# Adjacency loads of a two-layer graph attention kernel issued one row group at a time between GpSimd's node steps

## The chip, the core and the metric

One core of a Trainium2 chip runs the whole program. The metric is the device time of one execution in microseconds; the times given are of several executions of the same program, and lower is better.

## What is computed

Two graph attention layers with a pre-norm and a residual, over 8192 nodes of 128 features and one dense 0/1 adjacency of 8192 x 8192 int32 (268 MB):

```python
h = jnp.maximum(_layernorm(x, axis=-1), 0.0)
x = x + layer(h, adj, W, b, a)          # twice, with each layer's own weights
# layer:
Wh = h @ W + b
e = leaky_relu((Wh @ a1)[:, None] + (Wh @ a2)[None, :], 0.2)
attention = softmax(where(adj > 0, e, -9e15), axis=1)
return attention @ Wh
```

The adjacency is the same in both layers.

## The kernel before, in words

**The work of a tile.** Both layers go through 64 tiles of 128 target nodes. Since a leaky ReLU has two branches, a score's exponential is one of two products of a factor of the row and a factor of the column; so a tile needs only two masks of bits (edge and positive score, edge and negative score) and 128 matmuls (L560) of these masks, read as fp8, with 64 chunks of prepared node rows (`node_rows`), into two PSUM banks. VectorE makes the masks: two of four score signs (`z_sign`, L831), the AND with the edges (`mask_bits`, L846), the packing of the edges for layer 1 (`pack`, L872 and L875), a transposition (`turn_bits`, L884) and two splits (`split_g1`, `split_g2`, L891). ScalarE makes the other two score signs (L635) and, in layer 0 alone, turns the adjacency from int32 to an int8 sign (`cast`, L622, from `adj_sb` into `sign_a`). Layer 1 uses the packed edges and loads no adjacency.

**The adjacency's tile.** A tile of the adjacency, 128 rows of 8192 int32, is 4 MB and comes as four row groups r = 0 to 3 of 1 MB, each an indexed DMA on GpSimd's queue (`load_adj`, L422) that gathers 128 pieces of 2048 numbers. `adj_sb` has one place for each row group and no second one, so the load of group r of one tile may start once ScalarE has cast group r of the tile before (`cast_done`). After its four loads GpSimd steps the index (`adj_index`, L428).

**Node steps.** During layer 0, behind the matmuls of tile T+2, the nodes of tile T are prepared for layer 1. The chain goes over all engines: VectorE's mean and `centred` (L745) and `var_eps` (L748); GpSimd's `rstd` (`node_step`, L438); TensorE's transposition (`turn`, L507, at chunk 8 of 64) and projection (`project`, L512, at chunk 24); between them ScalarE's copy (`node_copy`, L597); then VectorE's `ext` (L812); then GpSimd's sum and copy of the two scores (`h_sum` L450 and `nat` L451), ScalarE's factors and first product (`node_high`, L608 and L610), GpSimd's second product (`row_parts`, L460), and VectorE's two remainders (`node_low`, L819), the first of which waits for ScalarE's product and the second for GpSimd's. SyncE stores the rows.

**The orders.** Every engine's order is written out by hand and repeats tile by tile. ScalarE, in the tile T+2 of layer 0, goes: `part_a` of the tile before (L641, waits for its matmuls), cast r = 0 of tile T+4, `node_copy` of T, z sign, cast r = 1, z sign, cast r = 2, `node_high` of T, cast r = 3. VectorE goes: z sign, `part_ac` (L911, waits for `part_a`), z sign, `joined`, `mask_bits`, `empty`, `pack`, `den` and `numer`, `turn_bits`, `ext` of T, `rden`, `split_g1`, `x_new`, `split_g2`, `stats` (L732), first `node_low` of T, `mean_var`, second `node_low` of T, `centred` and `var_eps` of T+1. GpSimd goes, for the nodes of T, through `load_adj` of all four groups of tile T+4, `node_step`, then `node_rest`, which has the sums and the second product. `sweep` (L91 to L105) writes 4 tiles out, loops over the middle and writes the last out.

Of the kernel before, what the change touches and what calls it, by code (L numbers as in the profile page):

```python
# [28 lines left out]
TILES = NODES // TILE  # L29
QUADS = 4  # L30
QROWS = 32
SPAN = NODES // QUADS
RGROUPS = TILE // QROWS
# [29 lines left out]
HEAD = 4  # L63
TAIL = 60
NODE_STEP = 4
LOADS_AHEAD = 4


class Tile:
# [24 lines left out]
def sweep(eng, body, trail=0, step=2, head=HEAD, tail=None):  # L94

    end = TILES - (tail or step)
    for k in range(head):
        body(Tile(k))
    with eng.Fori(head // step, end // step) as u:
        for k in range(step):  # L100
            body(Tile(k, u, step))
    for k in range(end, TILES + trail):
        body(Tile(k))


def gat_kernel(nc, x, adj, w_0, b_w_0, a_vec_0, b_a_0, w_1, b_w_1, a_1, out):
# [10 lines left out]
    with ExitStack() as ctx:  # L117
        def sb(name, shape, dt):
            return ctx.enter_context(nc.sbuf_tensor(name, shape, dt))
# [4 lines left out]
        def sem(name):  # L124
            return ctx.enter_context(nc.semaphore(name))


        adj_sb = sb("adj_sb", [128, RGROUPS, SPAN], I32)
        adj_index = sb("adj_index", [128, 2, RGROUPS], I32)
# [72 lines left out]
        adj_loaded = [sem(f"adj_loaded_{r}") for r in range(RGROUPS)]  # L202
        cast_done, index_ready = sem("cast_done"), sem("index_ready")
# [32 lines left out]
        def row_slot(l, T):  # L236

            return (T.p4, T.n4) if l == 0 else (T.p, T.n)
# [146 lines left out]
        @block.gpsimd  # L385
        def _(pool):
            pool.memset(minus_half[:], -0.5).then_inc(ident_ready, 1)
            pool.memset(averager[:], 1.0 / NODES).then_inc(ident_ready, 1)
            pool.memset(ident[:], 0.0).then_inc(ident_ready, 1)
            pool.wait_ge(ident_ready, 3)  # L390
            pool.affine_select(out=ident[:], in_=ident[:], compare_op=ALU.not_equal, fill=1.0, base=0,
                               pattern=[[-1, 128]], channel_multiplier=1).then_inc(ident_ready, 1)
            pool.wait_ge(ident_ready, 4)
            t_columns = ident[:, TILES:2 * TILES].rearrange("p (a b) -> p b a", a=QUADS)

            def build_picks():
                for r in range(RGROUPS):
                    pool.tensor_copy(pick_s[:, r, :].rearrange("p (a i) -> p a i", a=QUADS),
                                     ident[:, QROWS * r:QROWS * (r + 1)].unsqueeze(1).to_broadcast([128, QUADS, QROWS])) \
                        .then_inc(picks_ready, 1)  # L400
                for b in range(BLOCKS):
                    pool.tensor_copy(pick_t[:, b, :].rearrange("p (a i) -> p a i", a=QUADS),
                                     t_columns[:, b, :].unsqueeze(2).to_broadcast([128, QUADS, QROWS])).then_inc(picks_ready, 1)

            build_picks()
            pool.iota(adj_index[:].rearrange("p b r -> p (b r)"), pattern=[[QUADS * TILE, 2], [QUADS * QROWS, RGROUPS]], base=0,
                      channel_multiplier=QUADS).then_inc(index_ready, 1)
            pool.wait_ge(index_ready, 1)
            for a in range(1, QUADS):
                part = adj_index[QROWS * a:QROWS * (a + 1), :, :].rearrange("p b r -> p (b r)")  # L410
                pool.tensor_scalar(part, part, float(a - QUADS * QROWS * a), 1.0, ALU.add, ALU.mult).then_inc(index_ready, 1)
                pool.wait_ge(index_ready, a + 1)
            adj_rows_of_2048 = adj.rearrange("n (a c) -> (n a) c", a=QUADS)

            def load_adj(T):

                pool.wait_ge(index_ready, QUADS + T.t)
                for r in range(RGROUPS):
                    if T.u is not None or T.k:
                        pool.wait_ge(cast_done, RGROUPS * (T.t - 1) + r + 1)  # L420
                    pool.nop(nofuse=True)
                    pool.indirect_dma_start(out=adj_sb[:, r, :], out_offset=None, in_=adj_rows_of_2048,  # L422
                                            in_offset=bass.IndirectOffsetOnAxis(ap=adj_index[:, T.p, r:r + 1], axis=0)) \
                        .then_inc(adj_loaded[r], 16)
                if T.u is None and T.k == 0:
                    pool.engine_nop().then_inc(index_ready, 1)
                else:
                    pool.tensor_scalar(adj_index[:, 1 - T.p, :], adj_index[:, 1 - T.p, :], float(2 * QUADS * TILE), 1.0,  # L428
                                       ALU.add, ALU.mult).then_inc(index_ready, 1)

            nat_v = nat[:].rearrange("p (c t) -> p c t", c=2)

            def node_step(l, T):

                pool.wait_ge(S[l].var_eps, T.t + 1)
                T.wait_before(pool, S[l].ext, 2)
                pool.nop(nofuse=True)
                pool.tensor_tensor(rstd[:, T.p, :], var_eps[:, T.p, :], minus_half[:], ALU.pow).then_inc(S[l].rstd, 1)  # L438

            def node_rest(l, T):  # L440

                pool.wait_ge(S[l].ext, T.t + 1)
                if T.u is None and T.k == 0:
                    if l:
                        pool.wait_ge(S[0].h_mean, 1)
                    pool.tensor_copy(h_sum[:], ext[:, T.p, 0:DIM]).then_inc(S[l].h_sum, 1)
                else:
                    pool.wait_ge(S[l].h_sum, T.t)
                    pool.nop(nofuse=True)
                    pool.tensor_tensor(h_sum[:], h_sum[:], ext[:, T.p, 0:DIM], ALU.add).then_inc(S[l].h_sum, 1)  # L450
                pool.tensor_copy(nat_v[:, :, ds(T.t, 1)], ext[:, T.p, NEG_S:POS_T + 1].rearrange("p (c o) -> p c o", o=1)) \  # L451
                    .then_inc(S[l].st_kept, 1)
                if l == 0:
                    return
                pool.wait_ge(S[l].b_and_d, T.t + 1)
                slot, used = row_slot(l, T)
                if T.u is not None or used:
                    pool.wait_ge(S[l].rows_stored[slot], 16 * used)
                pool.nop(nofuse=True)
                pool.tensor_scalar(row_parts[:, slot, ROW:ROW + PART], ext[:, T.p, 0:PART], b_and_d[:, T.p, 1:2], 1.0,  # L460
                                   ALU.mult, ALU.mult).then_inc(S[l].high_d, 1)

            for l in range(LAYERS):
                if l:
                    load_adj(Tile(1))
                    pool.wait_ge(S[0].nat_ps, 1)
                    pool.wait_ge(S[0].coefs, 2)
                    pool.wait_ge(limits, n_limits)
                    for k in range(2, LOADS_AHEAD):
                        load_adj(Tile(k))  # L470

                def body(T):
                    if l and T.u is None and T.k == TILES - 2:
                        pool.wait_ge(S[0].turned, TILES)
                        build_picks()
                    if l == 0 and T.u is None and T.k == HEAD - 1:
                        load_adj(Tile(0))
                    if l and T.plus(LOADS_AHEAD).exists:
                        load_adj(T.plus(LOADS_AHEAD))
                    if T.exists:  # L480
                        node_step(l, T)
                    rest = T.plus(l - 1)
                    if rest.exists:
                        node_rest(l, rest)

                sweep(pool, body, trail=1 - l, step=[NODE_STEP, 2][l], tail=[NODE_STEP, LOADS_AHEAD][l])


        @block.tensor
# [804 lines left out]
```

## Time and profile before

| | us |
|---|---|
| median of 3 executions | 2281.99 |
| lowest, highest | 2279.98, 2282.03 |
| the profiled execution, its own time | 2267.0 |
| its span, first to last instruction | 2265.1 |
| layer 0's matmuls, about | 205 to 1310 of the span |
| layer 1's matmuls, about | 1335 to 2256 of the span |

| engine | busy us of the span |
|---|---|
| TensorE, matmul | 2016.6 (89%) |
| VectorE | 1778.2 (79%) |
| ScalarE | 1123.6 (50%) |
| GpSimd | 762.0 (34%) |

The busy shares are means over both layers, and the layers differ: only layer 0 has adjacency loads, casts and node steps. So the rows below are taken mainly from the stretch 280 to 1240 us, where layer 0 repeats itself tile by tile, and from single tiles in it. A release in square brackets at the end of a timeline row says how long the engine stood idle before the instruction and what it then waited for.

### The profile page before, as it was taken

The page shows a single profiled execution, that of the slowest core. Times are in us where ns is not written, and L with a number is a line of the kernel's source. Part 1 is how long each engine was busy: PE and PEld are TensorE (multiplying, and loading weights), DVE is VectorE, ACT ScalarE, POOL GpSimd, SP SyncE. Part 2 cuts the span into 40 slices and gives each one's busy share as a digit, 9 for nine tenths or more (in the row PEclk, how much of TensorE's full clock was granted, in tenths as well). Part 3 has the DMA queues.
Part 4 walks back from the last instruction along what each step waited for, and adds up shares of the span by engine and source line. Part 5 has one row for each costly group of instructions (what it writes and reads, how often), then busy time and mean ns, then how long its engine had stood idle before and what let it go on. Part 6 is the DMA issues. An engine that isn't in the chain of part 4 may idle for free.

```text
span 2265.1 us, 46517 instructions
## 1 busy us (share of the span) xinstructions
PE 2016.6 (89%) x16866; PEld 1708.1 (75%) x16866; DVE 1778.2 (79%) x2733; ACT 1123.6 (50%) x1097; POOL 762.0 (34%) x819
## 2 busy tenths in 40 slices
PE   4558888888888988889898969999999999999998
PEld 2337777777767777777777858888888888888887
DVE  5668787877778777787877768888888888888885
ACT  3467666676666766667676433332222222333331
POOL 5655565555656655565555410000000000000000
PEclk9999999999999999999999989999999999999999
DMA  5558777766777776776766570000000000000000
GB/s 184 138 170 284 262 271 271 270 239 257 266 263 270 268 264 256 263 276 261 273 259 258 197 164 29 28 28 28 28 28 28 28 28 28 28 28 28 27 27 11
DMA packets 104788, 357.40 MB, mean 158 GB/s; under 512 B 12336, under 2 KB 61744, under 8 KB 67888
## 3 DMA queue, kind: packets, MB, share of 16 engines
q0 software_dynamic: 36864, 268.45, 31.2%
q1 hardware_dynamic: 65584, 71.73, 11.3%
q10 hardware_dynamic: 2304, 16.78, 2.3%
q8 instruction: 18, 0.29, 0.1%
q14 instruction: 18, 0.15, 0.0%
HBM read 314.84 MB, written 42.07 MB: 158 GB/s over the span
## 4 chain that ended last, share of the span: by engine, by line
PE 47%; DMA 19%; ACT 14%; issue 14%; DVE 3%; POOL 1%; POOLq 0%; SPq 0%; DVEq 0%; ACTq 0%
PE acc L560 46%; DMA adj_sb<-in_adj_dram,adj_index 17%; ACT sign_a L622 8%; ACT sign_z L635 4%; DMA node_rows<-row_parts 2%; POOL adj_sb L422 1%; DMA masks<-in_x_dram 1%; ACT centred_t L597 1%; DVE ext L812 1%; PE ps_h L512 1%; PE acc L529 0%; ACT b_and_d L608 0%; DVE sign_z L846 0%; DVE masks L884 0%; ACT row_parts L610 0%
## 5 line engine op out<-in xcount | busy, mean ns | idle before, releaser
L560 PE MATMUL acc<-node_rows,masks 128*128 128x258 f16 x16384 | 1896.4, 277 | 26.0 <-DVE masks L891 13.0
L560 PEld LDWEIGHTS acc<-node_rows,masks 128*128 128x128 fp8e4 x16384 | 1622.8, 99 | 282.4 <-issue 16.4
L622 ACT ACTIVATE sign_a<-adj_sb 128x2048 int8<-128x2048 int32 x256 | 486.1, 1900 | 305.0 <-DMA adj_sb<-in_adj_dram,adj_index 300.7
L635 ACT ACTIVATE sign_z<-t_row,neg_s 128x2048 int8<-128x2048 f32 x256 | 503.9, 1994 | 2.0 <-DVE masks L884 1.9
L422 POOL DMA_INDIRECT adj_sb<-in_adj_dram,adj_index x256 | 447.3, 1747 | 121.6 <-issue 94.6
L641 ACT ACTIVATE part_a<-acc,coef_a 128x258 f32<-128x258 f32 x128 | 60.2, 471 | 710.1 <-PE acc L560 701.0
L831 DVE TENSOR_SCALAR sign_z<-t_row,neg_s 128x2048 int8<-128x2048 f32 x256 | 327.0, 1279 | 2.9 <-issue 2.4
L891 DVE TENSOR_SCALAR masks<-masks 128x2048 uint32<-128x2048 uint32 x256 | 311.7, 1217 | 0.3
L884 DVE STREAM_TRANSPOSE masks<-sign_z 128x2048 uint32<-128x2048 uint32 x128 | 294.9, 2304 | 0.1
L512 PE MATMUL ps_h<-w_ext,centred_t 128*128 128x133 f32 x256 | 85.8, 430 | 180.1 <-ACT centred_t L597 172.7
L819 DVE SCALAR_TENSOR_TENSOR row_parts<-ext,b_and_d,row_parts 128x129 f16<-128x129 f32 x256 | 90.4, 355 | 176.6 <-ACT row_parts L610 176.2
L911 DVE SCALAR_TENSOR_TENSOR part_ac<-acc,coef_c,part_a 128x258 f32<-128x258 f32 x128 | 62.1, 485 | 208.4 <-ACT part_a L641 202.7
L512 PEld LDWEIGHTS ps_h<-w_ext,centred_t 128*128 128x128 f32 x256 | 54.0, 263 | 211.5 <-ACT centred_t L597 159.8
L450 POOL TENSOR_TENSOR h_sum<-h_sum,ext 128x128 f32<-128x128 f32 x126 | 113.2, 899 | 191.8 <-DVE ext L812 188.1
L846 DVE SCALAR_TENSOR_TENSOR sign_z<-sign_z,pair_a 128x2048 uint32<-128x2048 uint32 x64 | 146.5, 2289 | 6.1 <-DVE pair_a L855 2.9
L846 DVE SCALAR_TENSOR_TENSOR sign_z<-sign_z,sign_a 128x2048 uint32<-128x2048 uint32 x64 | 146.3, 2285 | 3.5 <-ACT sign_z L635 3.2
L875 DVE SCALAR_TENSOR_TENSOR pair_a<-sign_a,pair_a 128x2048 uint32<-128x2048 uint32 x48 | 109.5, 2282 | 0.0
L460 POOL TENSOR_SCALAR row_parts<-ext,b_and_d 128x129 f16<-128x129 f32 x64 | 26.4, 412 | 211.4 <-ACT b_and_d L608 211.4
L438 POOL TENSOR_TENSOR rstd<-var_eps,minus_half 128x1 f32<-128x1 f32 x128 | 92.8, 726 | 10.1 <-DVE var_eps L748 4.8
L812 DVE SCALAR_TENSOR_TENSOR ext<-ps_h,rstd,bias 128x133 f32<-128x133 f32 x128 | 43.0, 336 | 36.5 <-PE ps_h L512 35.8
L608 ACT ACTIVATE b_and_d<-ext 128x2 f32<-128x2 f32 x128 | 25.3, 198 | 82.5 <-DVE ext L812 41.8
L507 PE MATMUL ps_t<-ident,centred 128*128 128x128 f32 x128 | 47.4, 372 | 19.6 <-DVE centred L745 18.3
(87 smaller groups left out, 695.5 us busy)
## 6 DMA issues: line engine op xcount, KB each, us to landing
node_rows<-row_parts SPq DMA_DIRECT2D x128, 129.0 KB, 2.2
node_rows<-node_rows SPq DMA_DIRECT2D x32, 516.0 KB, 11.7
mask_bytes<-pair_a ACTq DMA_DIRECT2D x16, 1024.0 KB, 4.9
pair_a<-mask_bytes SPq DMA_DIRECT2D x16, 1024.0 KB, 4.8
adj_sb<-in_adj_dram,adj_index POOLq DMA_INDIRECT x256, 9.0
x_old<-in_x_dram SPq DMA_DIRECT2D x64, 64.0 KB, 2.5
x_after_layer<-x_new SPq DMA_DIRECT2D x64, 64.0 KB, 2.9
x_old<-x_after_layer SPq DMA_DIRECT2D x64, 64.0 KB, 1.8
```

Source lines behind the costliest of these rows:

```text
L422: pool.indirect_dma_start(out=adj_sb[:, r, :], out_offset=None, in_=adj_rows_of_2048, in_offset=bass.IndirectOffsetOnAxis(ap=adj_index[:, ...
L438: pool.tensor_tensor(rstd[:, T.p, :], var_eps[:, T.p, :], minus_half[:], ALU.pow).then_inc(S[l].rstd, 1)
L450: pool.tensor_tensor(h_sum[:], h_sum[:], ext[:, T.p, 0:DIM], ALU.add).then_inc(S[l].h_sum, 1)
L512: pe.matmul(ps_h[:, 0:EXT], centred_t[:, T.p, :], w_ext[l][:], start=True, stop=True).then_inc(S[l].h_raw, 1)
L560: mm = pe.matmul(acc[T.p][s][:, 0:ROW], stationary[s][:, c // BYTES, c % BYTES, :], node_rows[:, c, ROW * s:ROW * (s + 1)], start=(c == 0) ...
L622: nc.scalar.activation(sign_a[:, T.p, SPAN * r:SPAN * (r + 1)], adj_sb[:, r, :], ACT.Sign, scale=-1.0) \
L635: nc.scalar.activation(sign_z[:, T.p, SPAN * r:SPAN * (r + 1)], t_row[:], ACT.Sign, scale=-1.0, bias=neg_s[:, ds(RGROUPS * T.t + r, 1)]).t ...
L831: nc.vector.tensor_scalar(sign_z[:, T.p, SPAN * r:SPAN * (r + 1)], t_row[:], neg_s[:, ds(RGROUPS * T.t + r, 1)], -1.0, ALU.is_gt, ALU.mult) \
L846: nc.vector.scalar_tensor_tensor(out=bits, in0=bits, scalar=LOW_Z_WORD[l][T.p4], in1=edges, op0=ALU.bitwise_xor, op1=ALU.bitwise_and).then ...
L875: nc.vector.scalar_tensor_tensor(out=pair, in0=edges, scalar=KEEP_WORD[T.p4], in1=pair, op0=ALU.bitwise_and, op1=ALU.bitwise_or).then_inc( ...
L884: nc.vector.transpose(g2[:, T.p, :].bitcast(U32).rearrange("p (b r i) -> p r b i", r=RGROUPS, i=QROWS), sign_z[:, T.p, :].bitcast(U32).rea ...
L891: return nc.vector.tensor_scalar(out, words, abs(left), EDGE_WORD, shift, ALU.bitwise_and)
```

## The change

`load_adj` now loads one row group and the step of the index is a function of its own. In layer 0, GpSimd's order for the nodes of T becomes: `node_step`, load r = 0 of tile T+5, the sums, loads r = 1 and r = 2, the second product (`node_high`), load r = 3, the step of the index. Tiles 1 to 4 are loaded before the first node step, in one piece each; before, these were tiles 1 to 3, and the load of tile 4 stood directly ahead of that node step. The waits of each load on the cast before it are the same as they were. The sweep for the first nodes, before layer 0, keeps its order, and the tail of the layer's sweep is written out for one pair of tiles more.

```diff
-LOADS_AHEAD = 4
+LOADS_AHEAD = 5
...
-            def load_adj(T):
-
-                pool.wait_ge(index_ready, QUADS + T.t)
-                for r in range(RGROUPS):
-                    if T.u is not None or T.k:
-                        pool.wait_ge(cast_done, RGROUPS * (T.t - 1) + r + 1)
-                    pool.nop(nofuse=True)
-                    pool.indirect_dma_start(out=adj_sb[:, r, :], out_offset=None, in_=adj_rows_of_2048,
-                                            in_offset=bass.IndirectOffsetOnAxis(ap=adj_index[:, T.p, r:r + 1], axis=0)) \
-                        .then_inc(adj_loaded[r], 16)
+            def load_adj(T, r):
+
+                if r == 0:
+                    pool.wait_ge(index_ready, QUADS + T.t)
+                if T.u is not None or T.k:
+                    pool.wait_ge(cast_done, RGROUPS * (T.t - 1) + r + 1)
+                pool.nop(nofuse=True)
+                pool.indirect_dma_start(out=adj_sb[:, r, :], out_offset=None, in_=adj_rows_of_2048,
+                                        in_offset=bass.IndirectOffsetOnAxis(ap=adj_index[:, T.p, r:r + 1], axis=0)) \
+                    .then_inc(adj_loaded[r], 16)
+
+            def advance_index(T):
...
+            def load_all(T):
+                for r in range(RGROUPS):
+                    load_adj(T, r)
+                advance_index(T)
...
-                def body(T):
...
-                    if l and T.plus(LOADS_AHEAD).exists:
-                        load_adj(T.plus(LOADS_AHEAD))
-                    if T.exists:
-                        node_step(l, T)
-                    rest = T.plus(l - 1)
-                    if rest.exists:
-                        node_rest(l, rest)
...
+                def layer_0_tile(T):
...
+                    later = T.plus(LOADS_AHEAD)
+                    node_step(1, T)
+                    if later.exists:
+                        load_adj(later, 0)
+                    node_sums(1, T)
+                    if later.exists:
+                        load_adj(later, 1)
+                        load_adj(later, 2)
+                    node_high(1, T)
+                    if later.exists:
+                        load_adj(later, 3)
+                        advance_index(later)
```

GpSimd's order in the loop over layer 0's tiles, before (the second of the loop's two tiles; `REGISTER_ALU` rows set up addresses, and names ending in `_1` in the brackets are the semaphores of layer 1's nodes):

```order
L458 REGISTER_ALU [waits b_and_d_1]
L460 TENSOR_SCALAR row_parts<-ext,b_and_d 128x129 [waits rows_stored_1_0]
L417 REGISTER_ALU
L420 ISA [waits index_ready]
L422 DMA adj_sb<-in_adj_dram,adj_index 128x2048 [waits cast_done]
L420 REGISTER_ALU
L422 DMA adj_sb<-in_adj_dram,adj_index 128x2048 [waits cast_done]
L420 REGISTER_ALU
L422 DMA adj_sb<-in_adj_dram,adj_index 128x2048 [waits cast_done]
L420 REGISTER_ALU
L422 DMA adj_sb<-in_adj_dram,adj_index 128x2048 [waits cast_done]
L428 TENSOR_SCALAR adj_index<-adj_index 128x4
```

All four loads stand behind the second product of the tile before, which waits for ScalarE's `b_and_d`.

The same place now (L446 is `rstd`, L458 and L459 are the sums, L469 the second product):

```order
L446 TENSOR_TENSOR rstd<-var_eps,minus_half 128x1 [waits var_eps_1,ext_1]
L418 REGISTER_ALU
L420 ISA [waits index_ready]
L422 DMA adj_sb<-in_adj_dram,adj_index 128x2048 [waits cast_done]
L458 TENSOR_TENSOR h_sum<-h_sum,ext 128x128 [waits ext_1,h_sum_1]
L459 ISA
L459 COPY nat<-ext 128x2
L420 REGISTER_ALU
L422 DMA adj_sb<-in_adj_dram,adj_index 128x2048 [waits cast_done]
L420 REGISTER_ALU
L422 DMA adj_sb<-in_adj_dram,adj_index 128x2048 [waits cast_done]
L469 TENSOR_SCALAR row_parts<-ext,b_and_d 128x129 [waits b_and_d_1,rows_stored_1_1]
```

The first load now stands ahead of the wait for `ext`, the next two ahead of the wait for `b_and_d`, and the fourth load and the index step follow behind the second product. No other engine's order changed.

## Rows read from the trace of the kernel before

**Rows 1.** The page: share of the chain that ended last.

```profile
PE 47%; DMA 19%; ACT 14%; issue 14%; DVE 3%; POOL 1%; POOLq 0%; SPq 0%; DVEq 0%; ACTq 0%
```

**Rows 2.** By stretch, layers 0 and 1: PE, PEld, DVE, ACT, POOL, PEclk, DMA share, GB/s.

```profile
280.00:1240.00 960.00, 836.83 (x7003) 707.65 (x7001) 755.56 (x1127) 651.48 (x535) 568.90 (x483) 0.95 0.71 266
1400.00:2265.00 865.00, 855.70 (x7634) 744.38 (x7631) 709.62 (x818) 244.15 (x174) 0.00 (x0) 1.00 0.08 26
```

**Rows 3.** Waits in 280 to 1240 us: us in total, times, longest us.

```profile
ACT sign_a L622 <- DMA adj_sb<-in_adj_dram,adj_index: 270.7, 54, 7.8
POOL row_parts L460 <- ACT b_and_d L608: 190.9, 53, 5.1
DVE row_parts L819 <- ACT row_parts L610: 135.1, 52, 4.1
PE ps_h L512 <- ACT centred_t L597: 123.2, 51, 5.5
...
DVE part_ac L911 <- ACT part_a L641: 33.0, 21, 2.6
```

**Rows 4.** Timeline of ScalarE in layer 0: start, duration, line, operation.

```profile
222.61 0.48 ACT L641 ACTIVATE part_a<-acc,coef_a 128x258 f32<-128x258 f32 x1 [1.39 <-PE acc L560]
...
1262.24 0.45 ACT L641 ACTIVATE part_a<-acc,coef_a 128x258 f32<-128x258 f32 x1
```

**Rows 5.** Timeline of one tile, GpSimd, ScalarE and VectorE mixed.

```profile
816.41 1.68 POOL L422 DMA_INDIRECT adj_sb<-in_adj_dram,adj_index  x1 [0.73 <-issue]
...
822.70 1.91 ACT L622 ACTIVATE sign_a<-adj_sb 128x2048 int8<-128x2048 int32 x1 [3.59 <-DMA adj_sb<-in_adj_dram,adj_index]
...
828.09 0.31 DVE L812 SCALAR_TENSOR_TENSOR ext<-ps_h,rstd,bias 128x133 f32<-128x133 f32 x1
...
828.58 1.34 POOL L450 TENSOR_TENSOR h_sum<-h_sum,ext 128x128 f32<-128x128 f32 x1 [2.20 <-DVE ext L812]
...
829.86 0.25 POOL L451 COPY nat<-ext 128x2 f32 x1
829.99 1.22 DVE L891 TENSOR_SCALAR masks<-masks 128x2048 uint32<-128x2048 uint32 x1
...
832.51 0.38 POOL L460 TENSOR_SCALAR row_parts<-ext,b_and_d 128x129 f16<-128x129 f32 x1 [2.40 <-ACT b_and_d L608]
...
833.39 1.60 POOL L422 DMA_INDIRECT adj_sb<-in_adj_dram,adj_index  x1 [0.50 <-issue]
```

**Rows 6.** Timeline of the next tile, VectorE and GpSimd.

```profile
833.09 0.32 DVE L819 SCALAR_TENSOR_TENSOR row_parts<-ext,b_and_d,row_parts 128x129 f16<-128x129 f32 x1
...
836.79 2.29 DVE L846 SCALAR_TENSOR_TENSOR sign_z<-sign_z,sign_a 128x2048 uint32<-128x2048 uint32 x1
837.10 2.79 POOL L422 DMA_INDIRECT adj_sb<-in_adj_dram,adj_index  x1 [0.31 <-issue]
...
843.82 0.31 DVE L812 SCALAR_TENSOR_TENSOR ext<-ps_h,rstd,bias 128x133 f32<-128x133 f32 x1
```

**Rows 7.** Groups of instructions in 280 to 1240 us.

```profile
L422 POOL DMA_INDIRECT adj_sb<-in_adj_dram,adj_index x214 | 386.3, 1805 | 83.3 <-issue 83.3
...
L875 DVE SCALAR_TENSOR_TENSOR pair_a<-sign_a,pair_a 128x2048 uint32<-128x2048 uint32 x40 | 91.3, 2282 | 0.0
...
L872 DVE TENSOR_SCALAR pair_a<-sign_a 128x2048 uint32<-128x2048 uint32 x14 | 17.2, 1226 | 4.7 <-DMA mask_bytes<-pair_a 4.7
```

**Rows 8.** Timeline of VectorE, one early tile without the load wait.

```profile
208.41 1.28 DVE L831 TENSOR_SCALAR sign_z<-t_row,neg_s 128x2048 int8<-128x2048 f32 x1
...
222.34 1.27 DVE L831 TENSOR_SCALAR sign_z<-t_row,neg_s 128x2048 int8<-128x2048 f32 x1
```

**Rows 9.** Timeline of TensorE, the same early tile.

```profile
209.78 0.27 PE L507 MATMUL ps_t<-ident,centred 128*128 128x128 f32 x1
...
224.43 0.27 PE L507 MATMUL ps_t<-ident,centred 128*128 128x128 f32 x1
```

**Rows 10.** The loads' tile: from issue to landing.

```profile
DMA to landing us min/median/max: 6.3/9.0/16.8
```

More of the change, by code:

```diff
@@ L438, in node_step, with node_sums @@
                 pool.tensor_tensor(rstd[:, T.p, :], var_eps[:, T.p, :], minus_half[:], ALU.pow).then_inc(S[l].rstd, 1)
-            def node_rest(l, T):
+            def node_sums(l, T):
                 pool.wait_ge(S[l].ext, T.t + 1)
@@ L452, in node_rest, with node_high @@
                     .then_inc(S[l].st_kept, 1)
-                if l == 0:
-                    return
+            def node_high(l, T):
                 pool.wait_ge(S[l].b_and_d, T.t + 1)
@@ L464, in _ @@
                 if l:
-                    load_adj(Tile(1))
+                    load_all(Tile(1))
                     pool.wait_ge(S[0].nat_ps, 1)
@@ L469, in _, with first_nodes @@
                     for k in range(2, LOADS_AHEAD):
-                        load_adj(Tile(k))
-                def body(T):
-                    if l and T.u is None and T.k == TILES - 2:
+                        load_all(Tile(k))
+                def first_nodes(T):
+                    if T.u is None and T.k == HEAD - 1:
+                        load_all(Tile(0))
+                    if T.exists:
+                        node_step(0, T)
+                    if T.plus(-1).exists:
+                        node_sums(0, T.plus(-1))
+                def layer_0_tile(T):
+                    if T.u is None and T.k == TILES - 2:
                         pool.wait_ge(S[0].turned, TILES)
                         build_picks()
-                    if l == 0 and T.u is None and T.k == HEAD - 1:
-                        load_adj(Tile(0))
-                    if l and T.plus(LOADS_AHEAD).exists:
-                        load_adj(T.plus(LOADS_AHEAD))
-                    if T.exists:
-                        node_step(l, T)
-                    rest = T.plus(l - 1)
-                    if rest.exists:
-                        node_rest(l, rest)
-                sweep(pool, body, trail=1 - l, step=[NODE_STEP, 2][l], tail=[NODE_STEP, LOADS_AHEAD][l])
+                    later = T.plus(LOADS_AHEAD)
[10 more added lines that the diff above has]
+                        advance_index(later)
+                if l == 0:
+                    sweep(pool, first_nodes, trail=1, step=NODE_STEP)
+                else:
+                    sweep(pool, layer_0_tile, tail=LOADS_AHEAD + 1)
         @block.tensor
```

## The prediction

> **What bounds the kernel now.** I read the chain that ended last first: 47% of it is TensorE and 19% is DMA [rows 1]. A DMA share on the chain is what a matmul-heavy kernel should not have, so I split the span by layer. In layer 1 TensorE is busy 855.70 of 865 us at clock 1.00; in layer 0 it is busy 836.83 of 960 us at 0.95 [rows 2]. Layer 1 has no loads and is TensorE's; nothing in the change touches it. Layer 0 is not bound by any engine's work: VectorE, the next busiest, has 755.56 us.
>
> The table of waits for the same 960 us says what it is bound by. ScalarE's cast waits 54 times, once a tile, for the adjacency: 270.7 us, 5.0 us a tile. GpSimd waits 190.9 us for ScalarE's `b_and_d` (L608, the factors that `node_high` computes), VectorE 135.1 us for ScalarE's `row_parts`, TensorE 123.2 us for ScalarE's `centred_t` [rows 3]. These are one loop. In one tile [rows 5]: GpSimd issues the load of group 0 at 816.41; it lands and the cast starts at 822.70, after ScalarE stood 3.59 us; ScalarE goes through its row of casts and signs to `b_and_d`, and only then comes GpSimd's product at 832.51, and behind that the next load of group 0 at 833.39. From load to load 16.98 us, of which some 6.3 us are a transfer that nothing covers. Group 0 had been cast by 824.61 (822.70 + 1.91), so the load that went out at 833.39 could have gone 8.8 us earlier.
>
> The rhythm of layer 0 over many tiles: ScalarE's `part_a` starts at 222.61 and at 1262.24, 58 tiles apart [rows 4], so 1039.63 / 58 = **17.92 us a tile**. All of the forecast is what takes the place of this number, times 58.
>
> **What the change does to the loop.** The load of group 0 is asked for ahead of the wait for `ext`, so as soon as its place is cast; from there to its use lies nearly a whole tile (needed about 16 us later, landing takes 6.3 at least and 9.0 in the median [rows 10]). Groups 1 and 2 go ahead of the wait for `b_and_d`. The count of instructions is the same: four loads and an index step a tile, none added, none removed, so nothing is gained or paid in work. The tiles loaded ahead of the first node step (1 to 4) have the same order as before, cost nothing, and what hides them is the end of the first nodes; if that cover were gone, it is once. The longer written-out tail repeats the same instructions: nothing. With the DMA wait out of the loop, three things could set the pace.
>
> *TensorE.* In an early tile where the cast was not waited for, turn to turn took 224.43 - 209.78 = 14.65 us [rows 9].
>
> *VectorE alone.* In the same tile z sign to z sign took 222.34 - 208.41 = 13.93 us [rows 8]. Each fourth tile packs with the short form, 1.23 instead of 2.28 us [rows 7]: a mean of 13.67.
>
> *VectorE behind GpSimd's product.* This is the new wait. Call X the start of `ext`. VectorE's second `node_low` needs GpSimd's product (L460), and this now stands behind the sums and two loads. The steps from the trace: the sums end at X + 2.02 (829.86 + 0.25 - 828.09) [rows 5]. About 0.4 us of issue, between the 0.30 between loads and the 0.50 and 0.73 ahead of a first load [rows 5], put load 1 at X + 2.4. There VectorE is in `split_g2`, which runs from X + 1.90 to X + 3.12 (829.99, 1.22) [rows 5]. A load that starts inside such an operation is held: the one at 837.10 started inside `mask_bits`, which ended at 839.08, and it ended 0.81 us after that, at 839.89 [rows 6]. By this row load 1 ends at X + 3.93. Load 2 starts 0.30 later and meets a VectorE with only small work left; no row of the groups above shows a load at such a place, so I bound it: from below 0.81, what the held load took once it was free [rows 6], above 1.81, the mean of 214 loads with all that holds them [rows 7]. I take 0.95, near the lower end, because VectorE there waits and holds nothing. It ends at X + 5.18; the product starts 0.1 later, takes 0.38 [rows 5], and ends at X + 5.66. The second `node_low` starts at X + 5.7. From that instruction to the next `ext` VectorE needed 843.82 - 833.09 = 10.73 us with no long wait in it [rows 6]. So the tile takes 16.43 us, less 0.26 for the short pack: **16.2 us**. That is above TensorE's 14.65, so this chain sets the pace: it is late next, where the transfer was.
>
> Bounds of this term. Lower: load 1 not held at all past `split_g2`, 0.7 us less: 15.5 us. Upper: both loads at the mean of 1.81 us: load 1 ends at X + 4.2, load 2 at X + 6.3, the product at 6.8, a tile of 17.3.
>
> A rule speaks to exactly this step. The Trainium skill, page "SBUF — State Buffer", section "A bandwidth-pool intuition that's wrong (but worth ruling out)", has a GpSimd DMA held until VectorE's end plus about 115 ns. The held row above shows 0.81 us after the end instead; by the rule the tile would take 15.5 us, an estimate that uses that page's figure, and by the row 16.2.
>
> **The sum.** 58 x (17.92 - 16.2) = 100 us. The profiled execution took 2267.0 us, so it would take 2167; the median of the three runs shown is 2281.99, 15 us above it, and I take the same 100 us off: **2182 us**.
>
> What hides the rest. ScalarE has 651.48 / 53.5 = 12.2 us of work a tile [rows 2, 7], so 4 us are free for a load that is late. Load 1 goes out at X + 2.4 and lands by X + 11.4 in the median [rows 10]; the cast wants it near X + 9, so it can wait 2 to 3 us, inside the slack. The traffic per tile, 0.71 x 17.92 = 12.7 us of all queues [rows 2, 4], fits into 16.2.
>
> **Rivals.**
>
> *A. GpSimd's product is in time and TensorE sets the pace:* 14.65 us a tile, 58 x 3.27 = 190 us less, 2092. For it: TensorE's own floor is that low [rows 9]. Against it: the sums, two loads of at least 0.81 us and the product can't end before X + 5, and VectorE has only small work left from X + 3.12.
>
> *B. The wait for the adjacency only moves to group 1 or to another group,* and the change does not do what it says: 0 us, 2282. It needs landings of over 12 us from issue. For it: the longest is 16.8 [rows 10]. Against it: the median is 9.0, with four loads close together, and now they are spread.
>
> *C. Slower: the two loads that stand ahead of the product are held by VectorE as the third load of a tile is now,* at 2.79 us [rows 6]. Load 1 would end at X + 5.2, load 2 at X + 8.3, the product at X + 8.8; the tile takes 19.3 us, 58 x 1.4 = 80 us more, 2362. It decides from the point where the two loads and their gap take 4.5 us rather than my 2.8 (the second `node_low` at X + 7.45). For it: the mean of all loads is already twice the free one [rows 7]. Against it: what held those were `mask_bits` and `pack`, and these don't stand between `ext` and `node_low`. The rule that speaks against this change stands on the page of the Trainium skill named above, section "SBUF: two separate sides": while VectorE runs an operation that takes both ports, GpSimd can't write a DMA's descriptors. Case C is what it would do here if such operations stood at this place.
>
> *D. The mean load:* as in the upper bound, 17.3 us, 0.6 x 58 = 35 us less, 2247. The forecast's own side, but its size is a third.
>
> **How the numbers follow.** Forecast (15.5 to 16.8 us a tile) 0.60; D 0.17; A 0.09; B 0.05; C 0.09. The range reaches from the lower bound, 58 x 2.4 = 140 us less, to a little above D: **2140 to 2252**. It leaves out A, B and C, 0.23, less what a mix of A and the forecast puts above 2140. Forecast, A and D are faster: 0.86; B is the same: 0.05; C slower: 0.09. About 0.2% is what a measurement of this kernel can tell from no change.
>
> **What would show it.** In the waits of the new trace, the cast's wait for the adjacency falls from 5.0 us a tile to under 1. VectorE's second `node_low` waits for GpSimd's product, about 2 us a tile, a wait that has no row among the long ones now; it is the core of the argument. TensorE's wait for `centred_t` falls under 1 us and its clock in layer 0 rises above 0.95. `part_a` comes every 16.2 us. Load 0 has long durations, up to 3.7 us, under `mask_bits` and `pack`, with nobody waiting. It would be wrong if the cast still waited (B), if nobody waited for the product (A), or if the loads ahead of it took 2 us and more (C, D).

## The result

| | median us | lowest, highest | runs |
|---|---|---|---|
| before | 2282.01 | 2279.98, 2283.51 | 4 |
| changed | 2169.37 | 2167.54, 2170.82 | 4 |

The ratio is 0.9507, with a 95% interval of 0.949 to 0.9523: faster by 113 us. The forecast was 2182, with a range of 2140 to 2252.

The profiled execution took 2170.76 us, 96 us less than the profiled one of before (2267.0). The medians differ by 113 us because the profiled execution of before was 15 us quicker than its own median, and that of the changed kernel was not. Where those 15 us come from is not known. In the three later comparisons, of the section on the experiments, all 26 executions of the kernel before took 2267.17 to 2277.16 us: they lie by the profiled one, and the four here above them. The comparison of traces below speaks of the 96.

### The profile page after: what moved, and what is told of

The parts are those of the page before. It is cut to its first block, busy times and chain, and to the rows that moved or that the text cites. A ratio compares the mean times of both kernels' runs of the same rounds, so it can differ in the third digit from the quotient of the medians.

```text
span 2169.0 us, 46499 instructions
## 1 busy us (share of the span) xinstructions
PE 1983.9 (91%) x16866; PEld 1682.5 (78%) x16866; DVE 1774.1 (82%) x2733; ACT 1137.9 (52%) x1097; POOL 759.1 (35%) x819
## 4 chain that ended last, share of the span: by engine, by line
PE 46%; issue 21%; DVE 11%; DMA 10%; POOL 5%; ACT 4%; DVEq 1%; POOLq 1%; SPq 0%; ACTq 0%
PE acc L583 45%; DMA adj_sb<-in_adj_dram,adj_index 6%; DVE masks L907 5%; POOL adj_sb L422 3%; ACT sign_a L645 2%; DMA node_rows<-row_parts 2%; DMA mask_bytes<-pair_a 1%; ACT sign_z L658 1%; DVE ext L835 1%; DVE part_ac L934 1%; POOL row_parts L469 1%; DMA masks<-in_x_dram 1%; DVE sign_z L854 1%; DVE numer L953 1%; PE acc L552 1%
## 5 line engine op out<-in xcount | busy, mean ns | idle before, releaser
L583 PE MATMUL acc<-node_rows,masks 128*128 128x258 f16 x16384 | 1871.8, 274 | 51.6 <-DVE masks L914 35.7
L583 PEld LDWEIGHTS acc<-node_rows,masks 128*128 128x128 fp8e4 x16384 | 1604.2, 98 | 300.4 <-issue 53.5
L422 POOL DMA_INDIRECT adj_sb<-in_adj_dram,adj_index x256 | 422.9, 1652 | 80.6 <-issue 51.2
L458 POOL TENSOR_TENSOR h_sum<-h_sum,ext 128x128 f32<-128x128 f32 x126 | 112.6, 893 | 350.5 <-DVE ext L835 346.7
L446 POOL TENSOR_TENSOR rstd<-var_eps,minus_half 128x1 f32<-128x1 f32 x128 | 144.1, 1127 | 9.8 <-DVE var_eps L771 4.9
L535 PE MATMUL ps_h<-w_ext,centred_t 128*128 128x133 f32 x256 | 75.8, 388 | 50.7 <-ACT centred_t L620 43.1
L530 PE MATMUL ps_t<-ident,centred 128*128 128x128 f32 x128 | 50.8, 398 | 60.1 <-DVE centred L768 58.8
L530 PEld LDWEIGHTS ps_t<-ident,centred 128*128 128x128 f32 x128 | 20.7, 162 | 94.3 <-DVE centred L768 68.2
L620 ACT COPY centred_t<-ps_t 128x128 f32<-128x128 f32 x128 | 32.4, 254 | 80.9 <-PE ps_t L530 80.8
```

The source lines that it names most:

```text
L535: pe.matmul(ps_h[:, 0:EXT], centred_t[:, T.p, :], w_ext[l][:], start=True, stop=True).then_inc(S[l].h_raw, 1)
L583: mm = pe.matmul(acc[T.p][s][:, 0:ROW], stationary[s][:, c // BYTES, c % BYTES, :], node_rows[:, c, ROW * s:ROW * (s + 1)], start=(c == 0) ...
```

## The profile after, and how it answers to the rows before

The page: span, TensorE's line, and the engines' shares of the chain that ended last.

```profile
span 2169.0 us, 46499 instructions
...
PE 1983.9 (91%) x16866; PEld 1682.5 (78%) x16866; DVE 1774.1 (82%) x2733; ACT 1137.9 (52%) x1097; POOL 759.1 (35%) x819
...
PE 46%; issue 21%; DVE 11%; DMA 10%; POOL 5%; ACT 4%; DVEq 1%; POOLq 1%; SPq 0%; ACTq 0%
```

DMA's share of the chain was 19% [rows 1] and is 10%; VectorE's was 3% and is 11%, GpSimd's 1% and 5%. Busy time by stretch (the stretch and its length in us, then the busy us of PE, PEld, DVE, ACT and POOL with their counts, the granted clock as a share of full speed, the DMA share, GB/s), layer 0 and layer 1:

```profile
280.00:1140.00 860.00, 801.22 (x6975) 680.17 (x6974) 744.45 (x1118) 660.30 (x532) 561.97 (x480) 0.99 0.78 292
1300.00:2160.00 860.00, 859.86 (x7670) 748.01 (x7668) 712.15 (x817) 247.11 (x176) 0.00 (x0) 1.00 0.08 26
```

In layer 0 TensorE is now busy 93% of the stretch at clock 0.99, where it was 87% at 0.95 [rows 2]. Layer 1 is as it was. The waits in layer 0's repeating part, 53 tiles:

```profile
engine line waited for: us in total, times, longest us
POOL h_sum L458 <- DVE ext L835: 244.1, 53, 8.1
DVE row_parts L842 <- POOL row_parts L469: 108.6, 53, 3.2
ACT b_and_d L631 <- DVE ext L835: 87.3, 41, 2.9
ACT centred_t L620 <- PE ps_t L530: 57.1, 53, 2.7
...
PE ps_t L530 <- DVE centred L768: 38.4, 52, 1.9
ACT sign_a L645 <- DMA adj_sb<-in_adj_dram,adj_index: 34.0, 32, 2.4
```

The wait of the cast for the adjacency, 270.7 us in 54 tiles [rows 3], is 34.0 in 53: 5.0 us a tile became 0.64. The second row is the one that did not stand among the long ones before: VectorE's second `node_low` waits 53 times for GpSimd's product, 108.6 us, 2.05 us a tile. TensorE waits at `turn` (L530), for `centred`, 0.7 us a tile; its wait of 123.2 us at `project` [rows 3] is gone. ScalarE now stands before `b_and_d` and before `node_copy` (L620), 2.7 us a tile in the two rows: it is early, where it was what the others waited for.

The pace, by the same two `part_a` rows, 58 tiles apart, that gave 17.92 us [rows 4]:

```profile
226.93 0.48 ACT L664 ACTIVATE part_a<-acc,coef_a 128x258 f32<-128x258 f32 x1 [1.38 <-PE acc L583]
...
1164.51 0.48 ACT L664 ACTIVATE part_a<-acc,coef_a 128x258 f32<-128x258 f32 x1 [0.22 <-PE acc L583]
```

937.58 / 58 = **16.17 us a tile**, so 102 us of layer 0 went. The trace has 96 in all because this execution reached the first of these rows 4.3 us later than that of before. It isn't the change: the same kernel in another execution, below, reached it at 222.91, against 222.61 before. Another 1.6 us were lost behind the second of these rows.

One tile, VectorE and GpSimd, as the timeline has it:

```profile
802.19 2.29 DVE L869 SCALAR_TENSOR_TENSOR sign_z<-sign_z,sign_a 128x2048 uint32<-128x2048 uint32 x1
802.89 2.48 POOL L422 DMA_INDIRECT adj_sb<-in_adj_dram,adj_index  x1 [0.19 <-issue]
...
804.45 2.29 DVE L898 SCALAR_TENSOR_TENSOR pair_a<-sign_a,pair_a 128x2048 uint32<-128x2048 uint32 x1
...
809.21 0.32 DVE L835 SCALAR_TENSOR_TENSOR ext<-ps_h,rstd,bias 128x133 f32<-128x133 f32 x1
...
809.71 1.32 POOL L458 TENSOR_TENSOR h_sum<-h_sum,ext 128x128 f32<-128x128 f32 x1 [4.33 <-DVE ext L835]
...
810.99 0.24 POOL L459 COPY nat<-ext 128x2 f32 x1
811.11 1.22 DVE L914 TENSOR_SCALAR masks<-masks 128x2048 uint32<-128x2048 uint32 x1
811.38 1.80 POOL L422 DMA_INDIRECT adj_sb<-in_adj_dram,adj_index  x1 [0.15 <-issue]
...
813.49 0.94 POOL L422 DMA_INDIRECT adj_sb<-in_adj_dram,adj_index  x1 [0.30 <-issue]
814.48 0.39 POOL L469 TENSOR_SCALAR row_parts<-ext,b_and_d 128x129 f16<-128x129 f32 x1
814.89 0.35 DVE L842 SCALAR_TENSOR_TENSOR row_parts<-ext,b_and_d,row_parts 128x129 f16<-128x129 f32 x1 [2.03 <-POOL row_parts L469]
...
815.04 1.78 POOL L422 DMA_INDIRECT adj_sb<-in_adj_dram,adj_index  x1 [0.18 <-issue]
...
815.42 1.28 DVE L854 TENSOR_SCALAR sign_z<-t_row,neg_s 128x2048 int8<-128x2048 f32 x1
...
819.12 2.89 POOL L422 DMA_INDIRECT adj_sb<-in_adj_dram,adj_index  x1 [0.19 <-issue]
...
820.67 1.22 DVE L895 TENSOR_SCALAR pair_a<-sign_a 128x2048 uint32<-128x2048 uint32 x1
```

Call the start of `ext` X, as the prediction does. With X = 809.21: the sums end at X + 2.02, load 1 takes 1.80, load 2 takes 0.94, the product ends at X + 5.66, and VectorE's second `node_low` starts at X + 5.68. In the sum it was X + 5.7. This tile is no exception: over 51 tiles in 280 to 1120 us the second `node_low` starts 5.68 us after `ext` on average. The last four rows, load 3 of this tile and load 0 of the next with the VectorE operations beside them, are read in the last section.

## The experiments

They change only the order of GpSimd's steps in layer 0; the last two also change when ScalarE issues a store. P is the theory of the prediction: the second `node_low` behind GpSimd's product sets the pace. L is the rival: the loads, or the transfers, still set it. They ran in three later comparisons, in which the kernel before had medians of 2272.06 us (first moved, one between, three ahead, first behind the sums), 2269.69 (two before the sums, first moved again, the changed kernel) and 2274.45 (the two with an early store). The changed kernel itself:

> The changed kernel itself on the chip of the experiments: 16.2 us a tile, 2160 to 2170, so that the orders are compared with it directly.

Measured: 2162.52 us (2159.69 to 2166.46), ratio to before 0.9528 (0.9515 to 0.9541), 16.08 us a tile. All tiles' lengths below are taken over the same 58 tiles as above, from one profiled execution of each kernel.

| order of a tile's steps on GpSimd (L0 to L3: loads 0 to 3) | loads between the sums and the product | median us | us a tile |
|---|---|---|---|
| changed: rstd, L0, sums, L1, L2, product, L3 | 2 loads | 2162.52 | 16.08 |
| three ahead: rstd, L0, sums, L1, L2, L3, product | 3 loads, index | 2260.13 | 17.75 |
| first behind the sums: rstd, sums, L0, L1, L2, product, L3 | 3 loads | 2241.75 | 17.39 |
| one between: rstd, L0, sums, L1, product, L2, L3 | 1 load | 2092.08 | 14.97 |
| only the first moved: rstd, L0, sums, product, L1, L2, L3 | none | 2085.39, 2090.22 | 14.86, 14.91 |
| two before the sums: rstd, L0, L1, sums, product, L2, L3 | none | 2115.76 | 15.36 |
| the same with an early store | none | 2076.08 | 14.65 |
| only the first moved, with an early store | none | 2082.55 | 14.76 |

### Only load 0 moved

```diff
                     node_step(1, T)
                     if later.exists:
                         load_adj(later, 0)
                     node_sums(1, T)
+                    node_high(1, T)
                     if later.exists:
                         load_adj(later, 1)
                         load_adj(later, 2)
-                    node_high(1, T)
-                    if later.exists:
                         load_adj(later, 3)
                         advance_index(later)
```

> Order for a tile's nodes: rstd, load 0, sums, product, loads 1 to 3. Only load 0 is still moved against the kernel before. Theory P (the second node_low waits for GpSimd's product, and this sets the tile's 16.17 us): the product ends 2.5 us after ext, VectorE no longer waits for it, and TensorE's floor of 14.65 us sets the pace; 14.65 to 14.9 us a tile, 58 x 1.4 = 81 us under the changed kernel's 2169, 2088, and the wait of node_low for GpSimd gone. Theory L (the loads set it, through the 34 us for which the casts still wait): loads 1 and 2 go out about as late as now or later, no gain, 2169 or slower, with longer waits of the casts.

Measured: 2085.39 us, ratio 0.9171 (0.9151 to 0.9191). Its waits in 280 to 1140 us:

```profile
ACT sign_a L646 <- DMA adj_sb<-in_adj_dram,adj_index: 130.3, 98, 4.2
...
POOL row_parts L469 <- ACT b_and_d L632: 58.2, 41, 4.2
...
DVE row_parts L843 <- ACT row_parts L634: 27.4, 20, 3.2
```

`node_low` has no wait for the product left in these 860 us. The product ends later than the 2.5 us after `ext` that were expected, 3.4 in the median of 51 tiles. The product waits for ScalarE instead, 58.2 us, which was 190.9 [rows 3]. The casts wait 130.3 us for the adjacency, nearly four times the 34.0 of the changed kernel, and the kernel is 3% faster: by far the most of the waits lie in ScalarE's slack. L falls; a small rest of it comes back with the last two runs.

Once more, beside the changed kernel in one comparison:

> The order where only load 0 is moved, once more beside the order with two loads ahead of the sums and beside the changed kernel, on one chip: 2085, and 0.96 of the changed kernel.

Measured: 2090.22 us, ratio to before 0.9204 (0.9189 to 0.9219), 0.967 of the changed kernel's median in the same comparison. This divides the change into its parts: moving load 0 alone is worth 179 us (2269.69 - 2090.22), and moving loads 1 and 2 as well gives 72 of them back (2162.52 - 2090.22).

### One load between

The edit is the one above with `load_adj(later, 1)` left ahead of `node_high`.

> Order: rstd, load 0, sums, load 1, product, loads 2 and 3. Theory P: the product ends 4.4 us after ext rather than 5.66; a full tile takes 4.5 + 10.56 = 15.1 us, one with the short pack stays at TensorE's 14.65; mean 14.95, 58 x 1.2 = 70 us under the changed kernel, 2099, and node_low waits some 0.8 us a tile. Theory L: no change, 2169.

Measured: 2092.08 us, ratio 0.9203 (0.9184 to 0.9222), 14.97 us a tile. The wait for the product is 0.7 us each, by its row in 280 to 1140 us:

```profile
DVE row_parts L843 <- POOL row_parts L469: 35.9, 49, 1.9
```

### Three loads ahead

```diff
                         load_adj(later, 1)
                         load_adj(later, 2)
-                    node_high(1, T)
-                    if later.exists:
                         load_adj(later, 3)
                         advance_index(later)
+                    node_high(1, T)
```

> Order: rstd, load 0, sums, loads 1, 2 and 3, product. The suspected wait is lengthened by a third load. Theory P: the product ends some 1.25 us later, 6.9 us after ext; 17.3 us a tile, 58 x 1.1 = 64 us over the changed kernel, 2233, and node_low waits 3.2 us a tile. Theory L: load 3 goes out earlier, so no change or a small gain, 2160 to 2169.

Measured: 2260.13 us, ratio 0.9948 (0.993 to 0.9967), 17.75 us a tile. GpSimd and VectorE in one tile (loads 2 and 3, the index step, the product, `node_low`):

```profile
805.67 1.28 POOL L458 TENSOR_TENSOR h_sum<-h_sum,ext 128x128 f32<-128x128 f32 x1 [5.44 <-DVE ext L836]
...
809.41 0.94 POOL L422 DMA_INDIRECT adj_sb<-in_adj_dram,adj_index  x1 [0.30 <-issue]
810.65 0.94 POOL L422 DMA_INDIRECT adj_sb<-in_adj_dram,adj_index  x1 [0.30 <-issue]
...
811.66 0.20 POOL L431 TENSOR_SCALAR adj_index<-adj_index 128x4 int32<-128x4 int32 x1
811.95 0.38 POOL L469 TENSOR_SCALAR row_parts<-ext,b_and_d 128x129 f16<-128x129 f32 x1
812.36 0.35 DVE L843 SCALAR_TENSOR_TENSOR row_parts<-ext,b_and_d,row_parts 128x129 f16<-128x129 f32 x1 [3.58 <-POOL row_parts L469]
```

and two of its waits in 280 to 1140 us:

```profile
DVE row_parts L843 <- POOL row_parts L469: 177.8, 49, 4.7
...
ACT sign_a L646 <- DMA adj_sb<-in_adj_dram,adj_index: 8.0, 12, 1.4
...
ACT sign_a L646 <- issue: 2.9, 12, 0.3
```

This is the clearest run of the study. The casts hardly wait for the adjacency, 8.0 us in all, less than a quarter of the changed kernel's 34.0, and yet the kernel is only 0.5% faster than before. The expected 17.3 us was too short by 0.4, of which 0.3 is the index step (0.20 and its gaps), which stood ahead of the product too and which I had left out of the expectation. Over 46 tiles in 280 to 1120 us the second `node_low` starts 7.25 us after `ext`, where the changed kernel has 5.68, and from there to the next `ext` a tile with the long pack takes 10.63, where that has 10.69: all of the lost time is ahead of `node_low`.

### Load 0 behind the sums

```diff
                     node_step(1, T)
-                    if later.exists:
-                        load_adj(later, 0)
                     node_sums(1, T)
                     if later.exists:
+                        load_adj(later, 0)
                         load_adj(later, 1)
                         load_adj(later, 2)
```

> Order: rstd, sums, loads 0, 1 and 2, product, load 3. Load 0 goes back behind the wait for ext, loads 1 and 2 stay ahead of the wait for b_and_d. Theory P: three loads stand ahead of the product, it ends about 7.0 us after ext; 17.3 us a tile, 2235, as in the order with three loads ahead, and ScalarE's late cast 0 (about 4 us later in the tile) is still hidden in its slack. Theory L: the cast of group 0 waits for a transfer in every tile again, 4 to 5 us, and the tile comes near the 17.92 us of the kernel before, 2270.

Measured: 2241.75 us, ratio 0.9882 (0.9846 to 0.9919), 17.39 us a tile (expected 17.3). In 280 to 1140 us:

```profile
ACT sign_a L646 <- DMA adj_sb<-in_adj_dram,adj_index: 236.8, 53, 7.5
DVE row_parts L843 <- POOL row_parts L469: 149.8, 49, 3.8
```

The casts' wait is back, 4.5 us each, as L expected. But the pace is P's: VectorE waits 3.06 us a tile for the product, 1 us more than in the changed kernel, and the tile is 1.3 us longer. The second `node_low` starts 6.98 us after `ext` on average (7.0 expected), and the way from there to the next `ext` is as long as in the changed kernel, 10.70 us in tiles with the long pack.

### Two loads ahead of the sums

```diff
                     if later.exists:
                         load_adj(later, 0)
+                        load_adj(later, 1)
                     node_sums(1, T)
+                    node_high(1, T)
                     if later.exists:
-                        load_adj(later, 1)
                         load_adj(later, 2)
-                    node_high(1, T)
-                    if later.exists:
                         load_adj(later, 3)
                         advance_index(later)
```

> Order: rstd, loads 0 and 1, sums, product, loads 2 and 3: the product as early as in the order where only load 0 is moved, and load 1 asked for before ext. Theory P: TensorE's floor of 14.65 us a tile sets the pace in both; the casts' waits for the adjacency fall from 130 us to under 80 in the same stretch, but they lay in ScalarE's slack, so the time is the same within 10 us, 2075 to 2085 on that chip. Theory L, in the weaker form that the waits of 130 us still cost the 0.2 us a tile above the floor: 14.65 us a tile, 12 us less, 2073.

Measured: 2115.76 us, ratio 0.9318 (0.9306 to 0.9331). A miss: 25 us slower than the order with only load 0 moved, though nobody waits for the product and the casts wait about as little as in the order with three ahead. In 280 to 1140 us:

```profile
DVE pair_a L896 <- DMA mask_bytes<-pair_a: 67.9, 14, 5.3
...
ACT sign_a L646 <- DMA adj_sb<-in_adj_dram,adj_index: 9.8, 13, 1.1
```

The first row is the new wait: each fourth tile, VectorE's `pack` may overwrite `pair_a` only when its 1 MB has been stored, and for that it waits 4.85 us in each of 14 tiles. The store's time from issue to landing (median, the last number), in this kernel and then in the one with only load 0 moved:

```profile
mask_bytes<-pair_a ACTq DMA_DIRECT2D x16, 1024.0 KB, 9.4
```

```profile
mask_bytes<-pair_a ACTq DMA_DIRECT2D x16, 1024.0 KB, 5.1
```

The order with only load 0 moved, run again, has 5.7. Both theories had left the store out. Theory M: ScalarE issues the store at the beginning of a tile, where loads 2 and 3 now come; it shares the DMA engines with them and takes 9.4 us rather than 5.1. One of the 14 stores, between the two loads, and the pack that waits for it:

```profile
835.38 1.94 POOL L422 DMA_INDIRECT adj_sb<-in_adj_dram,adj_index  x1 [0.17 <-issue]
...
837.18 0.34 ACTq L653 DMA_DIRECT2D mask_bytes<-pair_a  x1
...
846.28 1.23 DVE L896 TENSOR_SCALAR pair_a<-sign_a 128x2048 uint32<-128x2048 uint32 x1 [4.54 <-DMA mask_bytes<-pair_a]
```

All 14 stores start 0.1 to 0.3 us before GpSimd is through with issuing load 2, the first one behind the product. With only load 0 moved, that is load 1; there 2 of 14 stores start so, and theirs are the two longest waits, 5.2 and 4.2 us. That fits M, but that the loads make the store slow is argued from this order of issue, not measured by itself; what the next run tests is whether the late store is what costs the time.

### The store issued earlier

```diff
-                if T.p4 == PACK - 1 and (T.u is not None or T.k < TILES):
-                    store_pair(T)
...
                 if ahead.exists:
                     cast(ahead, 3)
+                if T.p4 == PACK - 2 and (T.u is not None or T.k < TILES):
+                    store_pair(T.plus(1))
```

With two loads ahead of the sums:

> Two loads ahead of the sums, and ScalarE issues the store of the packed edges at the end of the tile before, behind cast 3, some 3 to 4 us earlier against VectorE's next pack. Theory M (what the order with two loads ahead of the sums loses is the wait of VectorE's pack for this 1 MB store, 67.9 us in 14 tiles, because the store now runs beside loads 2 and 3): the wait falls to under 15 us, the mean tile from 15.36 to 14.7 us, 38 us less than that order, 2078. Rival (GpSimd's longer operations under VectorE's, the index step at 1.8 and rstd at 2.0 us, set that order's pace): no change, 2116.

Measured: 2076.08 us (2074.75 to 2076.98), ratio 0.9137 (0.9119 to 0.9155), 14.65 us a tile. Its wait for the store and its busy times in 280 to 1080 us:

```profile
DVE pair_a L895 <- DMA mask_bytes<-pair_a: 19.0, 13, 2.2
```

```profile
280.00:1080.00 800.00, 800.00 (x7154) 700.89 (x7153) 761.80 (x1149) 667.68 (x546) 680.21 (x493) 1.00 0.88 322
```

The wait is 1.5 us in 13 tiles instead of 4.85 in 14, and TensorE is busy 800.00 of 800 us at clock 1.00, with DMA at 0.88 of its engines' time. M holds in what it says of the cost: the late store cost this order 40 us (2115.76 - 2076.08), 38 expected. The rival, that GpSimd's held operations set that order's pace, falls, for these were left as they were and still take 1.7 and 1.9 us in the mean. But the store has not become quick, and 19.0 us of wait are more than the 15 expected:

```profile
806.38 0.34 ACTq L653 DMA_DIRECT2D mask_bytes<-pair_a  x1
...
816.43 1.23 DVE L895 TENSOR_SCALAR pair_a<-sign_a 128x2048 uint32<-128x2048 uint32 x1 [1.13 <-DMA mask_bytes<-pair_a]
```

From its issue to the pack that it lets go lie 10 us; without the wait there would be 8.9, where the late store had 4.6. What the edit gives is an earlier start, not a store clear of loads: now loads 0 and 1 are issued just ahead of it, load 1 until 0.4 to 1.2 us before it starts.

With only load 0 moved:

> Only load 0 moved, with the same early store. The pack waits 13 us for the store in that order. Theory M: gone, and the tile comes from 14.86 to 14.7 us: 10 us less, 2080. Rival: TensorE's floor holds both, no change within 5 us, 2088.

Measured: 2082.55 us, ratio 0.9163 (0.9145 to 0.9182), 14.76 us a tile. This one doesn't settle its question. The wait for the store did not go: it is 13.3 us in 11 tiles where it was 13.0 in 6. Its ratio to before, 0.9163, is below the two of the same order without the early store, 0.9171 and 0.9204, but these are one kernel and differ by 0.0033 among themselves. Whether the early store helps this order stays open; that the tile came from 14.86 to 14.76 us is too little to tell.

The last two kernels differ from each other only in load 1, ahead of the sums or behind the product, and ran in one comparison: 2074.75 to 2076.98 us against 2079.47 to 2083.4. So load 1 ahead of the wait for `ext` is worth 6.5 us, 0.3%. The casts' wait for the adjacency is 4.4 us in 280 to 1080 us there and 125.1 with only load 0 moved; that this wait is what costs the 6.5 us fits the weak form of theory L, but no run shows it by itself.

## Why the prediction was right

- **The bound of the kernel before.** Right: loads behind the wait for `b_and_d`. Taking load 0 alone out of the loop gave 179 us, more than the whole change.
- **The new wait.** Right, in place and in size: `node_low` waits for GpSimd's product 2.05 us a tile, "about 2" forecast; the product ends at X + 5.66 as summed.
- **Load 1 held by `split_g2`.** It started at 811.38 inside the operation of 811.11 and ended at 813.18, 0.85 us after that one's end at 812.33; the row of before had 0.81 [rows 6]. All 52 loads that started inside `split_g2` in 280 to 1140 us ended 0.85 to 0.87 us after it. The rule in the Trainium skill, page "SBUF — State Buffer", section "A bandwidth-pool intuition that's wrong (but worth ruling out)", would have it 115 ns after. For these loads the trace doesn't agree, and the row was the better guide: 16.2 us against 15.5, measured 16.17 and 16.08. For a load that VectorE's operation catches under way it does agree, as the last section shows.
- **Load 2 in a free place.** 0.95 us taken, 0.94 measured; the mean over all loads, 1.81, would have been wrong by a factor of two here. Case D rested on it. The 0.95 was a choice within bounds, but it could have been read from the trace of before, in the very tile of [rows 5], 2 us behind the first row there:

```profile
818.40 0.94 POOL L422 DMA_INDIRECT adj_sb<-in_adj_dram,adj_index  x1 [0.30 <-issue]
```

- **The lower bound.** "Not held at all past split_g2" is 0.81 us less by the held row, not 0.7, so 15.4 us a tile. Nothing hung on it.
- **TensorE's floor.** 14.65 us, read from one early tile [rows 9], is what the order with two loads before the sums and the early store reaches over 58 tiles, 14.65.
- **Signs of the forecast.** TensorE's wait for `centred_t` has no row among the long waits now, the clock rose to 0.99, the casts wait 0.64 us a tile, under 1. Wrong in a small thing: load 0 was to take up to 3.7 us under `mask_bits` and `pack`; at 802.89 it takes 2.48. It ended at 805.37, well within `pack`. The longest load of this stretch took 2.90, against 3.69 before.
- **The size.** 100 us forecast, 102 in the 58 tiles; the median fell by 113. The forecast took the 15 us by which the medians of before stood above its profiled execution to hold for the changed kernel too ("I take the same 100 us off"), and that did not hold: its median lies 1 us under its profiled execution, and 13 us under the forecast. Where before's profile and medians lie together, in the later comparison, 107 us went (2269.69 - 2162.52), which is 58 x (17.92 - 16.08).
- **The rivals.** A (the product in time, TensorE sets the pace) is not what this change does, but it is nearly what the order with only load 0 moved does: 190 us less in A, 187 and 179 measured, 14.65 us a tile in A, 14.86 and 14.91 measured. B fell. C fell too: it had both loads held, 2.79 us each, and they took 1.80 and 0.94. That time ahead of the product lengthens the tile, as C has it, is real: with a third load and the index step there the kernel is back at 17.75 us a tile, but with free loads and not with held ones.

What I did not ask while predicting is why loads 1 and 2 should move at all. The same chain of steps that gave 16.2 us comes out under TensorE's floor of 14.65 with the product ahead of them, so that the floor would set the pace; 14.9 was measured.

## What to carry to other kernels

When a load is issued by an engine that also does small steps for others, ask of each step on that queue who waits for it and how much slack that waiter has. A load moved ahead of a step takes its issue time, here 0.94 us free and 1.80 held, out of the slack of everybody behind that step. The load whose wait was on the loop earned it back many times over; the others did not, and were better left behind the product. The one place where another load was worth something, 6.5 us, was ahead of the sums, in time in which GpSimd waits for `ext` anyway. And before a transfer is moved, list the other transfers at its new time: the store that was hardly waited for, 4.7 us in 860, became the next bound.

## What the runs showed of the hardware that was not expected

What a load's issue on GpSimd takes beside VectorE depends on which of the two was first, and on VectorE's operation. All counts are of 280 to 1140 us in the changed kernel, where nothing else is said.

- With no long VectorE operation beside it, a load takes 0.94 us (54 loads, one of them 1.00).
- A load that starts inside `split_g2` or `mask_bits` is held and then takes nearly its whole time: it ends 0.85 to 0.87 us after the end of `split_g2` (52 loads), and 0.89 to 0.91 after that of `mask_bits` where the long pack follows (27 loads). The long pack, which follows at once, does not hold it: load 0 at 802.89 ended at 805.37, 0.89 us after `mask_bits` (804.48), while that pack ran from 804.45 to 806.74.
- The short pack does hold it: the 12 loads that started inside `mask_bits` ahead of a short pack ended 0.11 to 0.13 us after the pack's end. The load of 819.12 ended at 822.01, the pack of 820.67 at 821.89.
- A load that is under way when a z sign starts, and is still under way when that ends, ends 0.11 to 0.13 us after it: 40 of 53 loads, as the one of 815.04, which ended at 816.82 with the z sign's end at 816.70. The other 13 were through 1 us before. In the kernel before it is 97 of 99 loads in 280 to 1240 us, at 0.11 to 0.14.
- The transposition does not hold a load: with only load 0 moved, 51 loads started inside it and took 1.03 or 1.04 us.

Why the operations differ in this no run shows.
